# Moving the layernorm's normalize step from VectorE to GpSimd, and reordering the last four key tiles of attention

## The reference

```python
xn = _layernorm(x, axis=-1)                      # x: 4 x 2048 x 2048, f32
# attention: 16 heads of 128, q, k, v each divided by their L2 norm
scores = jnp.einsum('bhqd,bhkd->bhqk', q, k) * tau[0]
scores = jnp.where(causal, scores, -jnp.inf)
attn = softmax(scores) @ v * nu[0]
# experts: 32, top 8 of a softmax router, weights renormalized
g = jax.nn.silu(jnp.einsum('th,ehi->eti', xt, w_gate))
u = jnp.einsum('th,ehi->eti', xt, w_up)
y = jnp.einsum('eti,eih->eth', g * u, w_down)
ffn = jnp.einsum('eth,te->th', y, full_w)
x = x + attn + ffn
```

## Time and profile before

| what | value |
|---|---|
| time, median of 3 runs | 6587.74 us |
| the three runs | 6596.61, 6587.74, 5735.3 us |
| time of the profiled execution | 5733.36 us |
| span of its slowest core (core 4) | 5731.8 us |
| spans of the 8 cores | 5712.4 to 5731.8 us |
| TensorE busy | 5151.8 us (90%) |
| VectorE busy | 1667.3 us (29%) |
| GpSimd busy | 332.0 us (6%) |

### The profile page before, as it was taken

One profiled execution on the slowest core, in us unless ns is written; L12 is line 12 of the kernel. 1 busy time (PEld: TensorE's weight loads), 2 busy tenths in 40 slices (PEclk: granted clock), 3 DMA queues, 4 the chain that ended last, 5 costly groups with the idle time before them and its releaser, 6 DMA issues.

```text
span 5731.8 us, 59782 instructions; the slowest of 8 cores (5712.4 to 5731.8 us)
## 1 busy us (share of the span) xinstructions
PE 5151.8 (90%) x23180; PEld 2284.0 (40%) x23180; DVE 1667.3 (29%) x2573; ACT 741.0 (13%) x2033; POOL 332.0 (6%) x621
## 2 busy tenths in 40 slices
PE   4486979787599999999999999999999999999995
PEld 2231424232144444444444444444444444444443
DVE  2333444444322222222222222222222222222223
ACT  3323333333200000000000000000000000000000
POOL 0020100100000000000000000000000000000000
PEclk7687979888799999999999999999999999999997
DMA  3140211210144444333444454334444443344443
GB/s 80 56 53 7 30 15 16 30 15 1 20 70 75 73 85 87 70 67 67 74 74 74 84 88 72 67 67 74 74 74 81 88 74 67 67 72 75 74 81 132
DMA packets 89433, 365.21 MB, mean 64 GB/s; under 512 B 10948, under 2 KB 35780, under 8 KB 60484
## 3 DMA queue, kind: packets, MB, share of 16 engines
q0 software_dynamic: 84112, 327.39, 33.7%
q1 hardware_dynamic: 5044, 33.98, 1.7%
HBM read 680.17 MB, written 8.39 MB: 120 GB/s over the span
## 4 chain that ended last, share of the span: by engine, by line
PE 83%; DMA 5%; DVE 4%; ACT 4%; issue 3%; POOL 1%; ACTq 0%; DVEq 0%; SPq 0%; POOLq 0%
PE PQ L894 11%; PE PQ L893 11%; PE PQ L830 11%; PE PQ L833 11%; PE PQ L832 11%; PE PQ L831 11%; PE PQ L422 10%; DMA wd_sb<-wd 3%; PE PQ L547 2%; PE PQ L544 2%; PE PQ L567 2%; DMA x_sb<-x 1%; DVE acc L907 1%; ACT sq_junk L271 1%; PE PQ L389 1%
## 5 line engine op out<-in xcount | busy, mean ns | idle before, releaser
L830 PE MATMUL PQ<-xn_own,guw_sb 128*128 128x512 bf16 x3072 | 1164.7, 379 | 39.2 <-DVE acc L907 30.5
L832 PE MATMUL PQ<-xn_own,guw_sb 128*128 128x512 bf16 x3072 | 1164.8, 379 | 0.0
L831 PE MATMUL PQ<-xn_own,guw_sb 128*128 128x512 bf16 x3072 | 1164.7, 379 | 0.0
L833 PE MATMUL PQ<-xn_own,guw_sb 128*128 128x512 bf16 x3072 | 1164.6, 379 | 0.0
L894 PE MATMUL PQ<-gu_sb,wd_sb 128*128 128x512 bf16 x2880 | 1091.5, 379 | 0.0
L893 PE MATMUL PQ<-gu_sb,wd_sb 128*128 128x512 bf16 x2880 | 1091.5, 379 | 0.0
L851 DVE TENSOR_TENSOR gact<-gact,PQ 128x1024 bf16<-128x1024 bf16 x192 | 234.5, 1221 | 2355.7 <-ACT gact L844 2355.7
L907 DVE TENSOR_TENSOR acc<-acc,PQ 128x1024 f32<-128x1024 f32 x480 | 586.1, 1221 | 656.8 <-PE PQ L894 656.8
L844 ACT ACTIVATE gact<-PQ 128x1024 bf16<-128x1024 f32 x192 | 196.6, 1024 | 3834.7 <-PE PQ L833 3834.7
L830 PEld LDWEIGHTS PQ<-xn_own,guw_sb 128*128 128x128 bf16 x3072 | 300.7, 98 | 413.4 <-issue 55.0
L833 PEld LDWEIGHTS PQ<-xn_own,guw_sb 128*128 128x128 bf16 x3072 | 300.7, 98 | 362.9 <-issue 0.6
(11 more groups left out here) (112 smaller groups left out, 2594.2 us busy)
## 6 DMA issues: line engine op xcount, KB each, us to landing
guw_sb<-guw POOLq DMA_DIRECT2D x192, 1024.0 KB, 9.8
wd_sb<-wd POOLq DMA_DIRECT2D x192, 512.0 KB, 17.6
x_sb<-x SPq DMA_DIRECT2D x24, 1024.0 KB, 6.1
wt_sb<-wkt POOLq DMA_DIRECT2D x64, 128.0 KB, 8.3
wt_sb<-wvt POOLq DMA_DIRECT2D x64, 128.0 KB, 7.8
wt_sb<-wqt POOLq DMA_DIRECT2D x64, 128.0 KB, 8.1
out<-out_sb SPq DMA_DIRECT2D x8, 1024.0 KB, 4.8
wr_sb<-wT_sb POOLq DMA_DIRECT2D x32, 2.0 KB, 9.3
```

What stands on the lines that cost most here:

```text
L830: e.matmul(gp0[:], lhsT=lg, rhs=rx0, start=st_, stop=sp_)
L831: e.matmul(gp1[:], lhsT=lg, rhs=rx1, start=st_, stop=sp_)
L832: e.matmul(up0[:], lhsT=lu, rhs=rx0, start=st_, stop=sp_)
L833: last = e.matmul(up1[:], lhsT=lu, rhs=rx1, start=st_, stop=sp_)
```

## The change

It has two parts. In phase A, the instruction that normalizes a tile, `tensor_scalar` on 128x2048 f32, goes from VectorE's list to GpSimd's. GpSimd waits for VectorE's shift (`negmr`), and TensorE's transposes of that tile wait for GpSimd's semaphore in place of VectorE's. Reciprocal and shift remain on VectorE.

In attention, the key tiles are visited in the order 0 to 11, 14, 15, 12, 13, and slots, PSUM pairs, first and last flags of the accumulation and waits go by the position in that order instead of by kt.

```diff
-            pl.wait("tensor", "v", norm_v[i])
+            pl.wait("tensor", *norm_v[i])
...
                 e.reciprocal(rcol[par][:], stdb[par][:])
                 e.drain()
-                e.tensor_mul(negmr[par][:], negm[par][:], rcol[par][:])
+                e.tensor_mul(negmr[par][:], negm[par][:], rcol[par][:]).then_inc(SM["v"], 1)
+            pl.emit("vector", f_nm)
+            v_nmr = pl.inc("v")
+            pl.wait("gpsimd", "v", v_nmr)
+            def f_nm2(e, i=i, par=par):
                 e.drain()
                 e.tensor_scalar(x_sb[par][:], x_sb[par][:], rcol[par][:], negmr[par][:],
-                                ALU.mult, ALU.add).then_inc(SM["v"], 1)
-            pl.emit("vector", f_nm)
-            norm_v[i] = pl.inc("v")
+                                ALU.mult, ALU.add).then_inc(SM["g"], 1)
+            pl.emit("gpsimd", f_nm2)
+            norm_v[i] = ("g", pl.inc("g"))
...
+    KT_SEQ = list(range(12)) + [14, 15, 12, 13]
+    BANK_LAST = {}
+    for _kt in KT_SEQ:
+        a, b = qr_of(_kt)
+        if a < 512:
+            BANK_LAST[0] = _kt
+        if b > 512:
+            BANK_LAST[1] = _kt
...
-                    pT = pT_slots[kt % 4]
-                    st_ = kt == 0
+                    pT = pT_slots[pos % 4]
+                    st_ = pos == 0
...
-                        sp_ = kt == (11 if bk == 0 else NIC - 1)
+                        sp_ = kt == BANK_LAST[bk]
...
-            for kt in range(NIC):
-                pair = [P[0], P[1]] if kt % 2 == 0 else [P[2], P[3]]
-                if kt >= 2:
-                    pl.wait("tensor", "s", exp_s[kt - 2])
-                    if (kt - 2) in diag_v:
-                        pl.wait("tensor", "v", diag_v[kt - 2])
+            for pos, kt in enumerate(KT_SEQ):
+                pair = [P[0], P[1]] if pos % 2 == 0 else [P[2], P[3]]
+                if pos >= 2:
+                    pkt = KT_SEQ[pos - 2]
+                    pl.wait("tensor", "s", exp_s[pkt])
+                    if pkt in diag_v:
+                        pl.wait("tensor", "v", diag_v[pkt])
...
-                if kt >= 2:
-                    emit_av(kt - 2)
-            emit_av(NIC - 2)
-            emit_av(NIC - 1)
+                if pos >= 2:
+                    emit_av(KT_SEQ[pos - 2], KT_SEQ.index(KT_SEQ[pos - 2]))
+            emit_av(KT_SEQ[NIC - 2], NIC - 2)
+            emit_av(KT_SEQ[NIC - 1], NIC - 1)
```

More of the change, by code:

```diff
@@ L530, in build_nc, with emit_av @@
             diag_v = {}
-            def emit_av(kt, h=h, hh=hh):
+            def emit_av(kt, pos, h=h, hh=hh):
                 if kt >= 8:
@@ L536, in emit_av, with f_av @@
                     pl.wait("tensor", "s", exp_s[kt])
-                if kt == 0 and (h > 0 or g > 0):
+                if pos == 0 and (h > 0 or g > 0):
                     pl.wait("tensor", "v", attn_done[("epi", hh - 1)])
-                def f_av(e, h=h, kt=kt):
-                    pT = pT_slots[kt % 4]
-                    st_ = kt == 0
+                def f_av(e, h=h, kt=kt, pos=pos):
+                    pT = pT_slots[pos % 4]
+                    st_ = pos == 0
                     for (bk, a, b2) in spans(kt):
-                        sp_ = kt == (11 if bk == 0 else NIC - 1)
+                        sp_ = kt == BANK_LAST[bk]
                         e.matmul(P[4 + bk][:, a - bk * 512:b2 - bk * 512],
@@ L551, in emit_av @@
                 av_t[kt] = pl.inc("t")
-            for kt in range(NIC):
-                pair = [P[0], P[1]] if kt % 2 == 0 else [P[2], P[3]]
-                if kt >= 2:
-                    pl.wait("tensor", "s", exp_s[kt - 2])
-                    if (kt - 2) in diag_v:
-                        pl.wait("tensor", "v", diag_v[kt - 2])
-                if kt == 1 and (g > 0 or h > 0):
-                    pl.wait("tensor", "s", attn_done.get(("exp15", hh - 1), 0))
-                if kt == 0:
+            for pos, kt in enumerate(KT_SEQ):
[5 more added lines that the diff above has]
+                        pl.wait("tensor", "v", diag_v[pkt])
+                if pos == 1 and (g > 0 or h > 0):
+                    pl.wait("tensor", "s", attn_done.get(("exp_pong", hh - 1), 0))
+                if pos == 0:
                     pl.wait("tensor", "v", grp_ready_v)
                     if h > 0 or g > 0:
-                        pl.wait("tensor", "s", attn_done.get(("exp14", hh - 1), 0))
+                        pl.wait("tensor", "s", attn_done.get(("exp_ping", hh - 1), 0))
                 def f_sT(e, h=h, kt=kt, pair=pair):
@@ L587, in build_nc, with f_ex @@
                     pl.wait("scalar", "t", sT_t[kt])
[L588 to L594, removed]
+                if pos >= 4:
+                    pkt4 = KT_SEQ[pos - 4]
+                    pl.wait("scalar", "t", av_t[pkt4])
+                    if pkt4 in mask_v:
+                        pl.wait("scalar", "v", mask_v[pkt4])
+                def f_ex(e, kt=kt, pos=pos):
+                    pT = pT_slots[pos % 4]
+                    pq = PQ[0] if pos % 2 == 0 else PQ[1]
                     a, b2 = qr_of(kt)
@@ L603, in build_nc, with f_mk @@
                     pl.wait("vector", "s", exp_s[kt])
-                    def f_mk(e, kt=kt):
-                        pT = pT_slots[kt % 4]
+                    def f_mk(e, kt=kt, pos=pos):
+                        pT = pT_slots[pos % 4]
                         e.drain()
@@ L612, in build_nc @@
                     mask_v[kt] = pl.inc("v")
-                if kt == 2 and pending_epi:
+                if pos == 2 and pending_epi:
                     flush_epi()
-                if kt >= 2:
-                    emit_av(kt - 2)
-            emit_av(NIC - 2)
-            emit_av(NIC - 1)
-            attn_done[("exp14", hh)] = exp_s[NIC - 2]
-            attn_done[("exp15", hh)] = exp_s[NIC - 1]
-            pl.wait("vector", "t", av_t[NIC - 1])
+                if pos >= 2:
+                    emit_av(KT_SEQ[pos - 2], KT_SEQ.index(KT_SEQ[pos - 2]))
+            emit_av(KT_SEQ[NIC - 2], NIC - 2)
+            emit_av(KT_SEQ[NIC - 1], NIC - 1)
+            attn_done[("exp_ping", hh)] = exp_s[KT_SEQ[NIC - 2]]
+            attn_done[("exp_pong", hh)] = exp_s[KT_SEQ[NIC - 1]]
+            pl.wait("vector", "t", av_t[KT_SEQ[NIC - 1]])
             if pending_rb_t[0]:
```

## The result

| what | before | changed |
|---|---|---|
| median of 26 runs each | 5928.11 us | 5953.92 us |
| shortest run | 5735.3 us | 5715.12 us |
| ratio, undisturbed runs alone | | 0.9946 [0.9919, 0.9973] |
| ratio, second comparison on one chip (e9 below) | | 0.9971 [0.9958, 0.9984] |

The account below looks back on a forecast made before the run. The prediction took phase A to be bound by a serial round through ScalarE, VectorE and TensorE, with the normalize delaying the copy. It summed 5733.4 - 19.05 - 5 = 5709 us, range 5693 to 5735 us.

Parts of the forecast that it names:

- the forecast is for the kind that was profiled: Whole kernel: forecast applies to executions like the profiled one, 5733.4 us, not the two long runs with median 6587.74 us.
- The normalize leaves VectorE: Phase A: the copy follows the shift directly, 1.27 us earlier in 15 tiles, so 19.05 us leave the chain.
- The clock in phase A: Phase A projections: shorter rounds move the clock step, so 5.5 us instead of 5.83 each, 5 us gained.
- The normalize on GpSimd: Phase A: the instruction takes 3 us on GpSimd (ends 1.35 and 4.7), hidden by about 16 us of cover.
- Tile 0: Head of phase A: first normalize on GpSimd could start at 19.2 us, with 4.5 us of cover, enough for 3 us.
- The order of key tiles: Attention: visiting 14, 15, 12, 13 last gives each position the same work, cost 0.
- What can shift later: Experts: load meetings with the neighbour core may change the wait for `wd`, 16 us the slowest core may gain or lose.
- better loads: Rival in the experts: the neighbour's loads come out better, 16 us less waiting, 5693 us; chance 0.07.
- the saved time is not the chain's: Rival in phase A: another wait takes the normalize's place, no change, 5733 us; chance 0.06.
- not side by side: Rival in phase A: GpSimd's instruction holds up VectorE's second copy, 5740 us at 3 us, 5765 at 4.7; chance 0.07.
- The clock takes it back: Rival in phase A: all projections last 6.54 us, costing 11 us of the 19, 5725 us; chance 0.08.
- GpSimd on the chain: Rival in phase A: GpSimd's instruction passes 16 us and delays the copy, break-even 19 us, slower; chance 0.02.

Follow-up runs that it names:

- e9: The changed kernel as it is, timed and profiled a second time; ratio to the kernel before 0.9971 [0.9958, 0.9984].
- e10: The changed kernel without the drain ahead of each normalize on GpSimd, timed against the kernel before; ratio 0.999 [0.994, 1.004], cores 5688.3 to 5709.0 us.
- e7: The changed kernel with four more value-preserving instructions of the same size after each GpSimd normalize; phase A rounds of 17.10 us.
- e8: The changed kernel with nine more value-preserving instructions after each GpSimd normalize; phase A rounds of 21.04 us, spans 5775.7 to 5817.7 us.
- e5: The kernel before with the new order of key tiles alone, normalize still on VectorE; profiled run 5735.04 us.
- e6: The changed kernel with key tiles back in their old order, so the normalize on GpSimd alone; ratio to the kernel before 0.999 [0.9967, 1.0014].
- e1: The changed kernel with only the drain ahead of each normalize on GpSimd taken away; 5710.57 us.
- e3: The changed kernel with 8 more 128 KB loads behind GpSimd's first 16; first normalize at 35.74 us instead of 29.73 in core 4.
- e4: The changed kernel with tile 0 alone normalized on VectorE; undisturbed cores 4 to 7 span 5690.6 to 5710.8 us.

## Why the prediction was right or wrong

The forecast was 5709 us with a range of 5693 to 5735. The median measured, 5953.92 us, lies far outside. The step behind that is the last of the sum, *the forecast is for the kind that was profiled*: two of the three runs shown were of the other kind, and the prediction gave it neither a time nor a chance. It is no effect of the change, since the kernel before is at 5928.11 us in as many runs; what makes an execution one of the long kind stays open. Against the profiled execution of before, the ratios give 5733.4 x 0.9971 = 5717 us and 5733.4 x 0.9946 = 5702 us, one 8 us above and one 7 us below the forecast, both in the range. The direction was right. The chances gave 0.97 to a change within 2%, and it is.

*The normalize leaves VectorE*, 15 x 1.27 = 19.05 us: the mechanism was right, both factors were a little off. The copy follows the shift directly in each round, but gains 1.41 us, with VectorE's `drain` (above). And of the first of the 15 only 0.4 us on average are gained, since projection 0 waits for its weights: in e10, without any delay on GpSimd, it starts at 28.2 to 30.0 us, and before it did at 29.0 to 30.5. So it is 14 x 1.41 = 19.7 us. The load of x kept its slack: in e9 it was issued at 170.5 us and landed 5.8 us later, before its reader at 178.7 us.

*The clock in phase A*, 5 us gained: the direction was right, the size too large. The rounds give 0.17 us each, some 2 us in 13 rounds. That the round came out at 17.0 us as forecast (from 18.62) is luck: the copy gave 0.14 us more than priced and the clock 0.16 us less. What was taken for a spread between 4.91 and 6.54 became nearly one value, 5.5 to 5.7 us; that it would was not foreseen.

*The normalize on GpSimd*, 3 us taken, 1.35 and 4.7 as ends: it takes 2.05 us. The element price from the two memsets (1.9 us) was the nearest row. The Trainium skill's ratio ("GPSIMD Engine Reference", Performance versus the Vector engine), 1.96 for a two-input add, gave 2.6 us; here the ratio is 2.05 / 1.35 = 1.5 for an instruction with one large input. The cover hid it either way: 10.3 us still disappear (e7), 20.5 us do not (e8).

*Tile 0*: this is the step of the mechanism that failed. The prediction put it so: *GpSimd is free by then: its 16 loads last 8.5 us and begin right after the constants*, and *the added wait on GpSimd holds back no other work, so it costs nothing*. The 8.5 us are the time to issue the loads; they landed up to 17.7 us after issue. The edit issues a second instruction on GpSimd besides the normalize, a drain, and the prediction gave it no price. It costs 10.59 us once, of which 7.0 us reach the projection of tile 0. In core 4: +7.0 at the head, 15.59 - 19.48 = -3.9 in the first round (1.4 of it the copy's, the rest since projection 0 takes 3.63 us in place of 6.51), 13 x -1.58 = -20.5 in the others, together -17.4 us (291.29 to 273.84), and the core's span is 16.2 us shorter. On average over the eight cores, where projection 0 is that short in three only, it is +7.2, -2.8 and -20.4, together -16.0 us, and for e10 -23.1 us. Without the drain (e10) the slowest core is 5709.0 us, 22.8 us under before. The forecast's gain was 24, near it in part because the errors of the two terms above cancel.

*The order of key tiles*, 0: right, as far as the trace and the undisturbed halves of e5 and e6 can tell.

*What can shift later*: one core of each neighbouring pair waits for `wd` 15 us or more in the kernel before, in e1 and in e5, and the other 6 us or less; in e9 it is 22.2 us in core 4 and 0.8 us in core 5. The slowest core of these kernels is one of those that wait, so the term neither helped nor hurt, and *better loads* did not come true.

Of the rivals, *the saved time is not the chain's* and *not side by side* fell with the lines of e9: the second copy isn't late. By the Trainium skill ("SBUF — State Buffer", Who interferes with whom), a VectorE instruction with at most one SBUF input, outside the two-port modes, doesn't contend with GpSimd. These lines agree for the copy out of PSUM: 0.69 us and 1.34 us with GpSimd running, as without. *The clock takes it back* fell, and *GpSimd on the chain* was true for tile 0 alone, by another mechanism than the one priced.

## What to carry to other kernels

An instruction that stands in an engine's list between a chain's link and its successor costs the chain its length even if nothing on the chain needs its result, and so does a drain that goes with it. Moving both to an idle engine gains the time from the link to its successor, here 1.41 us, so long as the work stays within the distance to its reader. When work goes to a queue that also issues loads, price each instruction that goes along, drains above all: ask what they wait for, and look up when the loads land, not when they were issued. And look for what else lands at that time: here the next step of the chain waits for the same loads, so only the work that the drain pushes behind them is lost.

## What the runs showed of the hardware

A drain on GpSimd waits for the transfers that GpSimd has issued: 10.59 us behind 17 loads, some 6 us more with 8 more loads, 0.2 us between the shift and the normalize without the drain. The instruction behind it starts 0.9 us after the last of the 16 loads of weights has landed (e9, all eight cores), 1.2 us after the last of the 8 more (e3). With no load out, it costs about 0.2 us.

A `tensor_scalar` of 128x2048 f32 with two columns as scalars takes 2.05 us on GpSimd, against 1.35 us on VectorE, and with constants as scalars 1.90 us (e7).

From tile 1 on in phase A the granted clock is at 1.2 GHz (0.50) when a projection begins and at 2.4 GHz (1.00) when it ends, in both kernels; in core 4 of e9 it is 0.50 from 188.0 to 192.5 us and 1.00 from 193.0 us, in the projection that starts at 188.9 us. With rounds of 18.6 us on average, projections alternated between 5.3 and 6.5 us; in the changed kernel, e1, e4, e6 and e7, whose rounds are 17.0 to 17.1 us, they lie between 5.5 and 5.7 us from tile 6 on; in e8, with rounds of 21 us, they last from 3.6 to 6.1 us. So the length of a round goes with the place at which the clock rises in it, and with 0.17 us of its own length here. Why it does so, no run shows.
